# Attention block on one core: the softmax reciprocals go through DRAM, and VectorE divides out of PSUM

## The chip, the cores and the metric

The kernel runs on one core of a Trainium2 chip. A core has TensorE (PE, matrix products into PSUM), VectorE (DVE), ScalarE (ACT) and GpSimd (POOL), each with its own instruction stream, and SyncE (SP), which here issues all DMAs from one queue in its written order. The engines meet only at semaphores. The metric is the device time of one execution in microseconds. Three runs of the kernel before took 717.3, 717.02 and 719.97 us; the median is 717.3 us.

## The reference

```python
q = (x @ Wq.T).reshape(B, N, 12, 32); k = (x @ Wk.T).reshape(...); v = (x @ Wv.T + bv).reshape(...)
a = einsum('bnhd,bmhd->bhnm', q, k) * SCALE + adj[:, None]     # adj is the bias of all heads
a = where(all(a == 0, axis=-1)[..., None], -inf, a)            # rows of zeros count as empty
a = nan_to_num(softmax(a, axis=-1))
o = einsum('bhnm,bmhd->bnhd', a, v).reshape(B, N, 384)
out = layernorm(x + (o @ Wo.T + bo), axis=-1)                  # B = 32 batches, N = 256 rows, float32
```

The softmax denominator is applied after the product with v: `o` is first computed with unnormalised exponentials and then multiplied by the reciprocal of each row's sum.

## The kernel before, in words

There are 32 independent batches of 256 rows and 384 columns, 12 heads of 32 columns. Every large float32 product is done as three products of a high and a low part (hi·hi, hi·lo, lo·hi). The order on each engine is written out by hand in three functions: `start()` (batches 0 to 2 and the beginning of 3), `step(t)`, run once for each batch in the middle, and `end()`. Engines work on neighbouring batches at once: t is the batch of a step, `prev`, `prev2`, `nxt` and `nxt2` are those one or two before or after it.

Pieces of one batch on TensorE, by the names used below:

- **K** blocks, three a batch: `project_kq` (K01, K2Q0, Q12), 18 matmuls of 256 columns each, into bank_c or bank_b.
- **V** blocks, two a batch: `project_v`, 9 matmuls of 384 columns into bank_b; **Y** blocks, two a batch: `project_y`, the output projection, the same shape from `o_hi`, `o_lo`.
- **S** blocks, three a batch: `scores(t, g)` for four heads each, into the four s_banks. VectorE then adds the bias and negates (`add_bias(t, u)`, L1192: units u = 0 to 11, two instructions each), and ScalarE takes the exponentials and the row sums (`exps`, L559).
- **T** blocks, four a batch: `transposes` of units 8 to 11 by the identity into bank_t, copied out by ScalarE (`copy_probT`). Units 0 to 7 are turned by VectorE in 32x32 squares (`square`, L1209), stored to DRAM and loaded again in turned order (`store_squares`, `load_squares`, 1 MB each, one pair for each of the head groups 0 and 1).
- **W** blocks, three a batch: `weigh(t, g)`, exponentials times v for head group g, into the first half of bank_a. All three groups use the same place, so each must be emptied before the next begins.
- **flag**: one small product that tells whether any row maximum is zero; VectorE reads it (`read_flag`, L1240), and `mask` (L1248) loads it into a register and branches over code that is not needed.

The reciprocals before: VectorE takes the 24 reciprocals of each partition, 12 heads by two halves of the rows (`invert`, L1264), GpSimd widens them to 32 columns each (`widen_inv`, L418), and TensorE turns them by six transposes (`spread`, L858: four into bank_c, two into bank_t). ScalarE copies each W result out of bank_a (`save_o`, L576), and VectorE multiplies that copy by the spread reciprocals in two instructions (`divide`, L1273). bank_a is free as soon as ScalarE has copied it (semaphores `o_saved`). Then `split_o_hi` (ScalarE) and `split_o_lo` (GpSimd) make the parts for Y, `residual` and `moments` (VectorE), `deviation` (GpSimd) and `normalise` (ScalarE) finish the batch.

Of the kernel before, what the change touches and what calls it, by code (L numbers as in the profile page):

```python
# [13 lines left out]
P = 128  # L14
# [66 lines left out]
def build(nc, x, xT, adj, wqT, wkT, wvT, bv, woT, bo, out):  # L81
    def sb(name, shape, dt=F32):
# [23 lines left out]
    sums = [sb(f"sums{p}", [P, NT, H]) for p in range(2)]  # L106
# [15 lines left out]
    most = sb("most", [P, NT, H])  # L122
    inv = sb("inv", [P, NT, H])
    inv_wide = sb("inv_wide", [P, NT, H, HD])
    o_raw = [sb(f"o_raw{p}", [P, KC, N]) for p in range(2)]
    o_n = sb("o_n", [P, KC, N])
# [19 lines left out]
    bank = {"R0": bank_c, "K01": bank_c, "Q12": bank_c, "PV0": bank_a, "PV1": bank_a, "PV2": bank_a,  # L146
            "K2Q0": bank_b, "V0": bank_b, "V1": bank_b, "Y0": bank_b, "Y1": bank_b}
    t_flat = bank_t[:].rearrange("p k m q -> p (k m q)")
    bank["R1"] = t_flat
    flags_at = bank_a[:, N:N + NT * H]  # L150
# [3 lines left out]
    last_bank = {"R0": s_flat[0], "Y0": s_flat[0], "R1": s_flat[1], "Y1": s_flat[1], "PV1": s_flat[2], "PV2": bank_c[:]}  # L154
# [42 lines left out]
    o_saved = [sem(f"o_saved{g}") for g in range(KC)]  # L197
# [4 lines left out]
    inv_wide_ready = sem("inv_wide_ready")  # L202
    inv_spread = sem("inv_spread")
# [11 lines left out]
    CONSTS = 4  # L215
# [7 lines left out]
    with nc.Block() as block:  # L223

        @block.sync
        def _(sp):
# [32 lines left out]

            def store_out(t):  # L260
# [27 lines left out]
            def start():  # L288
                t0 = Batch(0)
                t1 = Batch(1)  # L290
                t2 = Batch(2)
                t3 = Batch(3)
                t4 = Batch(4)
                load_bias(t1)
                load_xt(t2)
                load_xr(t0)
                store_squares(t0, 0)
                load_xr(t1)
                load_squares(t0, 0)
                load_xt(t3)  # L300
                store_squares(t0, 1)
                load_xt(t4)
                load_squares(t0, 1)
                load_bias(t2)
                store_squares(t1, 0)
                store_squares(t1, 1)
                load_squares(t1, 0)
                load_squares(t1, 1)
                load_bias(t3)
                store_squares(t2, 0)  # L310
                load_squares(t2, 0)
                load_xr(t2)
                store_squares(t2, 1)
                load_bias(t4)
                load_squares(t2, 1)
                store_squares(t3, 0)
                store_out(t0)

            def step(t):
                nxt2 = t.later(2)  # L320
                nxt = t.later(1)
                prev2 = t.later(-2)
                load_xt(nxt2)
                load_bias(nxt2)
                load_squares(t, 0)
                store_squares(t, 1)
                load_squares(t, 1)
                load_xr(t)
                store_squares(nxt, 0)
                store_out(prev2)  # L330

            def end():
                t28 = Batch(28)
                t29 = Batch(29)
                t30 = Batch(30)
                t31 = Batch(31)
                store_squares(t30, 1)
                load_squares(t30, 0)
                load_squares(t30, 1)
                store_squares(t31, 0)  # L340
                load_xr(t30)
                load_squares(t31, 0)
                store_squares(t31, 1)
                store_out(t28)
                load_squares(t31, 1)
                store_out(t29)
# [5 lines left out]
            for c in range(3, 30):  # L352
                step(Batch(c))
# [4 lines left out]
        def _(pool):  # L358
# [3 lines left out]
            pool.wait_ge(const_ready, 3)  # L362
# [41 lines left out]
            def split_o_lo(t, k):  # L404
# [5 lines left out]
                nc.gpsimd.tensor_tensor(o_lo[:, a:b], o_n[:, a:b], o_hi[:, a:b].bitcast(F32), ALU.subtract  # L410
                                        ).then_inc(o_ready, 1)

            def widen_inv(t):
                pool.wait_ge(inv_ready, t.count(1, 1))

                after(pool, inv_spread, t.count(2))
                apart(pool)
                nc.gpsimd.tensor_copy(inv_wide[:], inv[:].unsqueeze(3).to_broadcast([P, NT, H, HD])  # L418
                                      ).then_inc(inv_wide_ready, 1)
# [19 lines left out]
            def start():  # L439
# [9 lines left out]
                split_kq(t0, "Q12")  # L449
                permute_bias(t1)  # L450
                split_kq(t1, "K01")
                split_xt(t2)
                split_kq(t1, "K2Q0")
                split_kq(t1, "Q12")
                split_kq(t2, "K01")
                widen_inv(t0)
                split_kq(t2, "K2Q0")
                split_kq(t2, "Q12")
                permute_bias(t2)
                split_xt(t3)  # L460
                add_bo(t0)
                split_xt(t4)
                split_o_lo(t0, 0)
                split_kq(t3, "K01")
                split_o_lo(t0, 1)
                widen_inv(t1)
                split_kq(t3, "K2Q0")
                permute_bias(t3)
                add_bo(t1)
                split_kq(t3, "Q12")  # L470
                deviation(t0)
                widen_inv(t2)
                split_o_lo(t1, 0)
                split_kq(t4, "K2Q0")

            def step(t):
# [4 lines left out]
                permute_bias(nxt)  # L481
                split_o_lo(prev2, 1)
                split_kq(nxt, "K01")
                add_bo(prev)
                split_xt(nxt2)
                split_kq(nxt, "Q12")
                deviation(prev2)
                split_kq(nxt2, "K2Q0")
# [1066 lines left out]
```

## Time and profile before

| | |
|---|---|
| median of three runs | 717.3 us |
| the profiled execution's own time | 718.51 us |
| span of the profile | 716.2 us |
| PE busy, of the span | 698.7 us (98%) |
| DVE busy | 600.1 us (84%) |
| ACT busy | 613.8 us (86%) |
| POOL busy | 487.2 us (68%) |
| DMA packets, share of the 16 engines | 72.3% on SP's queue |
| HBM traffic | 256 GB/s over the span |

The span is the first to the last instruction; the execution's own time is 2.3 us more. PE's busy time counts pipelined matmuls, which overlap, so its work is best read as the distance from one block's start to the next block's start. The rows below have times in us from the span's start. In the timeline, the first number is the start, the second the time busy, and brackets hold idle time before the row and what ended it.

### The profile page before, as it was taken

To read this page: it belongs to the slowest core of one execution; us is meant where nothing else is said; L and a number is where in the kernel's file an instruction comes from. 1 tells how busy PE (TensorE), PEld (TensorE's weight loads), DVE (VectorE), ACT (ScalarE), POOL (GpSimd) and SP (SyncE) were. 2 spreads that over 40 slices of the span, in tenths; PEclk is the share of its full clock that TensorE was granted. 3 is DMA by queue.
4 is the path that set the end of the run, shared out by engine and by line. 5 is a ranking of instruction groups with operands and counts; after the bars stand their busy time and mean duration, and the time that the engine had idled before them with its cause. 6 is when DMAs were issued, how large, how long until landed. Compare 5 with 4: busy or idle time off the path is not lost.

```text
span 716.2 us, 23143 instructions
## 1 busy us (share of the span) xinstructions
PE 698.7 (98%) x7557; PEld 600.7 (84%) x7557; DVE 600.1 (84%) x2220; ACT 613.8 (86%) x1993; POOL 487.2 (68%) x548
## 2 busy tenths in 40 slices
PE   8999999999999999999999999999999999999895
PEld 8878888888888888888888888888898888888774
DVE  4898988889888889888889888889888889888973
ACT  4889988889988889988888988889888888898882
POOL 4767666677766678766677766678766677766452
PEclk9999999999999999999999999999999999999998
DMA  8475877787777687777787777787777777777672
GB/s 266 152 278 206 300 267 264 252 315 236 263 263 273 241 309 240 265 264 267 251 302 240 262 267 259 252 305 247 257 270 261 262 291 248 255 273 259 248 288 90
DMA packets 84008, 184.61 MB, mean 258 GB/s; under 512 B 4272, under 2 KB 42928, under 8 KB 75696
## 3 DMA queue, kind: packets, MB, share of 16 engines
q1 hardware_dynamic: 83888, 183.12, 72.3%
q8 instruction: 61, 1.00, 0.6%
q14 instruction: 59, 0.48, 0.2%
HBM read 103.42 MB, written 79.69 MB: 256 GB/s over the span
## 4 chain that ended last, share of the span: by engine, by line
PE 85%; DVE 5%; DMA 4%; issue 2%; POOL 2%; ACT 1%; SPq 0%; DVEq 0%; ACTq 0%; POOLq 0%
PE bank_b L787 34%; PE bank_c L787 16%; PE bank_a L877 12%; PE s_bank L836 11%; PE bank_t L847 8%; PE bank_c L858 2%; DVE neg L1192 2%; DMA sq_dram<-w_f 2%; DMA sq_probT<-sq_dram 2%; ACT prob L559 1%; PE bank_t L858 1%; DVE w_f L1209 1%; DMA xt<-in_xT 1%; POOL kq_lo L400 0%; DVE y L1292 0%
## 5 line engine op out<-in xcount | busy, mean ns | idle before, releaser
L559 ACT ACTIVATE prob<-neg,negmax 128x256 f32<-128x256 f32 x768 | 380.3, 500 | 51.8 <-DVE w_f L1209 34.3
L1192 DVE CUSTOM_DVE_ANT_0 neg<-s_bank,bias_sq 128x256 f32<-128x256 f32 x512 | 185.2, 414 | 49.0 <-issue 42.6
L1209 DVE STREAM_TRANSPOSE w_f<-prob 128x512 f32<-128x512 f32 x256 | 173.2, 696 | 0.7 <-ACT prob L559 0.7
L559 ACT ACTIVATION_READ_ACCUMULATOR prob<-neg,negmax 128x1 f32 x768 | 147.7, 192 | 0.0
L400 POOL TENSOR_TENSOR kq_lo<-kq,kq_hi 128x512 fp32r<-128x512 f32 x96 | 125.2, 1304 | 7.7
L398 POOL CAST kq_hi<-kq 128x512 fp32r<-128x512 f32 x96 | 60.2, 627 | 79.3 <-issue 73.9
L787 PE MATMUL bank_c<-xt_hi,w_hi 128*128 128x256 f32 x384 | 111.1, 289 | 1.0 <-DVE w_lo L1171 1.0
L787 PE MATMUL bank_c<-xt_hi,w_lo 128*128 128x256 f32 x384 | 108.3, 282 | 0.0
L787 PE MATMUL bank_c<-xt_lo,w_hi 128*128 128x256 f32 x384 | 108.3, 282 | 0.0
L1192 DVE CUSTOM_DVE_ANT_0 neg<-s_bank,bias 128x256 f32<-128x256 f32 x256 | 91.0, 420 | 15.2 <-PE s_bank L836 15.0
L847 PE MATMUL bank_t<-ident,prob 128*128 128x128 f32 x512 | 80.3, 279 | 0.7 <-ACT probT L569 0.7
L569 ACT ACTIVATE probT<-bank_t 128x512 f32<-128x512 f32 x128 | 75.0, 586 | 3.6 <-PE bank_t L847 2.9
L787 PEld LDWEIGHTS bank_c<-xt_hi,w_hi 128*128 128x128 f32 x384 | 73.0, 190 | 2.1 <-issue 1.7
L410 POOL TENSOR_TENSOR o_lo<-o_n,o_hi 128x512 fp32r<-128x512 f32 (+1 forms) x62 | 63.4, 1025 | 15.4 <-ACT o_hi L584 15.4
L787 PEld LDWEIGHTS bank_c<-xt_hi,w_lo 128*128 128x128 f32 x384 | 73.1, 190 | 0.0
L787 PEld LDWEIGHTS bank_c<-xt_lo,w_hi 128*128 128x128 f32 x384 | 73.1, 190 | 0.0
L877 PE MATMUL bank_a<-sq_probT,v 128*32 128x256 f32 x1008 | 67.5, 385 | 1.2 <-DVE zero_flag L1240 1.0
L787 PE MATMUL bank_b<-w_hi,o_hi 128*128 128x384 f32 x186 | 68.3, 367 | 0.3 <-DVE y L1292 0.3
L787 PE MATMUL bank_b<-w_hi,xt_hi 128*128 128x384 f32 x192 | 67.8, 353 | 0.3 <-ACT kq L542 0.2
L836 PE MATMUL s_bank<-kq_hi 32*128 32x256 f32 x768 | 65.2, 328 | 2.6 <-POOL kq_lo L400 1.3
L836 PEld LDWEIGHTS s_bank<-kq_hi 32*128 32x128 f32 x768 | 37.3, 183 | 34.4 <-issue 33.3
L847 PEld LDWEIGHTS bank_t<-ident,prob 128*128 128x128 f32 x512 | 56.5, 140 | 10.7 <-issue 1.6
(88 smaller groups left out, 1794.1 us busy)
## 6 DMA issues: line engine op xcount, KB each, us to landing
sq_dram<-w_f SPq DMA_DIRECT2D x64, 1024.0 KB, 4.5
sq_probT<-sq_dram SPq DMA_DIRECT2D x64, 1024.0 KB, 5.6
xt<-in_xT SPq DMA_DIRECT2D x32, 384.0 KB, 4.5
xr<-in_x SPq DMA_DIRECT2D x32, 384.0 KB, 6.2
out_y<-y_out SPq DMA_DIRECT2D x31, 384.0 KB, 3.0
bias<-in_adj SPq DMA_DIRECT2D x32, 256.0 KB, 3.2
w_f<-in_wkT SPq DMA_DIRECT2D x3, 192.0 KB, 4.5
w_f<-in_wqT SPq DMA_DIRECT2D x3, 192.0 KB, 5.0
```

The costliest lines, as they stand in the source:

```text
L398: nc.gpsimd.tensor_copy(kq_hi[t.p][:, a:a + 2, :], kq[:, a:a + 2, :]).then_inc(kq_hi_ready[name], 1)
L400: nc.gpsimd.tensor_tensor(kq_lo[t.p][:, a:a + 2, :], kq[:, a:a + 2, :], kq_hi[t.p][:, a:a + 2, :].bitcast(F32), ALU.subtract).then_inc(kq_ ...
L410: nc.gpsimd.tensor_tensor(o_lo[:, a:b], o_n[:, a:b], o_hi[:, a:b].bitcast(F32), ALU.subtract).then_inc(o_ready, 1)
L559: nc.scalar.activation(prob[:, u % PROB_RING, k], neg[:, h, w.c], ACT.Exp, scale=-1.0, bias=negmax[t.p][:, w.c, h:h + 1], accum_out=sums[t ...
L569: nc.scalar.activation(probT[:, a:a + PAIR, :, P * w.c:P * (w.c + 1)], bank_t[:], ACT.Copy).then_inc(probT_act, 1)
L787: last = nc.tensor.matmul(ps, w_pair[a](k), m_pair[b](k), start=(k == 0 and e == 0), stop=(k == KC - 1 and e == 2))
L836: last = nc.tensor.matmul(s_bank[j][:, c, :], a[t.p][rows, KC + g, P * c:P * (c + 1)], b[t.p][rows, g, :], start=(e == 0), stop=(e == 2))
L847: last = nc.tensor.transpose(bank_t[:, k, m, :], prob[:, u % PROB_RING, k, P * m:P * (m + 1)], ident[:])
L858: last = nc.tensor.transpose(bank_at(t, f"R{k}")[:, at:at + P], inv_wide[:, c, JH * g:JH * (g + 1), :].rearrange("p h d -> p (h d)"), iden ...
L877: last = nc.tensor.matmul(bank_at(t, f"PV{g}")[HD * j:HD * (j + 1), 0:N], v[t.p][:, m, HD * h:HD * (h + 1)], weights, start=(m == 0), stop ...
L1192: nc.vector.tensor_tensor_reduce(out=neg[:, h, w.c], in0=s_bank[h % JH][:, w.c, :], in1=by[t.p][:, w.c, :], scale=-1.0, scalar=BIG, op0=AL ...
L1209: nc.vector.transpose(sq_stage[w.g][:, :, a:a + PAIR, :, w.c].rearrange("p b h m s -> p (h m) b s"), prob[:, u % PROB_RING].rearrange("p k ...
```

## The change

The spreading of the reciprocals leaves TensorE and GpSimd. `invert` now writes the 24 reciprocals into the first columns of a 32-column tile whose rest holds ones; `turn_inv` turns that in 32x32 squares on VectorE, so that a partition holds 32 rows of one head and one row half; `store_inv` writes the 16 KB to DRAM, where the rows of one head then lie in a line; and four loads (`load_inv`), one for each head position j, repeat 768 reciprocals over 32 partitions each and fill `inv_all`. `sums` has another order of its axes to suit that.

ScalarE's copy of the W results is gone. VectorE's `divide(t, g)`, now one instruction for each of the three groups, reads bank_a itself, so bank_a is free only when VectorE has divided. `o_n` has two buffers. The flag product goes to bank_t in place of bank_a. VectorE adds the bias of v in both kernels. All hand-written orders are new: `step` runs for batches 3 to 28 in place of 3 to 29, group 0 of a batch is weighed a step later, and xT is loaded three batches ahead.

```diff
-    inv_wide = sb("inv_wide", [P, NT, H, HD])
-    o_raw = [sb(f"o_raw{p}", [P, KC, N]) for p in range(2)]
-    o_n = sb("o_n", [P, KC, N])
+    inv = sb("inv", [P, SQ])
+    inv_t = sb("inv_t", [P, SQ])
+    inv_dram = [nc.dram_tensor(f"inv_dram{p}", (SQ, BLOCKS, SQ), F32, kind="Internal").ap() for p in range(2)]
+    inv_all = [sb(f"inv_all{p}", [P, KC, N]) for p in range(2)]
+    o_n = [sb(f"o_n{p}", [P, KC, N]) for p in range(2)]
...
-    flags_at = bank_a[:, N:N + NT * H]
+    flags_at = t_flat[:, 0:NT * H]
...
+            def store_inv(t):
+                sp.wait_ge(inv_turned, t.count(1, 1))
+                apart(sp)
+                after(sp, inv_loaded[t.p], JH * (t.loads() - DMA))
+                sp.dma_start(inv_dram[t.p].rearrange("k b r -> b k r"),
+                             inv_t[:]).then_inc(inv_stored[t.p], DMA)
+
+            def load_inv(t):
+                sp.wait_ge(inv_stored[t.p], t.loads())
+                apart(sp)
+                after(sp, o_n_ready, t.count(KC, -KC))
+                for j in range(JH):
+                    row = inv_dram[t.p][KC * NT * j:KC * NT * (j + 1)].rearrange("k b r -> (k b r)")
+                    sp.dma_start(inv_all[t.p][HD * j:HD * (j + 1)].rearrange("p g n -> p (g n)"),
+                                 row.rearrange("(a n) -> a n", a=1).to_broadcast([HD, KC * N])
+                                 ).then_inc(inv_loaded[t.p], DMA)
...
-            def widen_inv(t):
...
-            def save_o(t, g):
...
-            def spread(t, k):
...
             def invert(t):
                 dve.wait_ge(prob_ready, t.count(H * NT, H * NT))
-                after(dve, inv_wide_ready, t.count(1))
-                nc.vector.reciprocal(inv[:], sums[t.p][:]).then_inc(inv_ready, 1)
-
-            def divide(t, k):
-                a, b = ((0, 2), (2, 3))[k]
-                for g in range(a, b):
-                    dve.wait_ge(o_saved[g], t.count(1, 1))
-                after(dve, o_ready, t.count(2))
-                dve.wait_ge(inv_spread, t.count(2, k + 1))
-                nc.vector.tensor_tensor(o_n[:, a:b, :], o_raw[t.p][:, a:b, :],
-                                        bank_at(t, f"R{k}")[:, 0:N * (b - a)].rearrange("p (a n) -> p a n", n=N),
-                                        ALU.mult).then_inc(o_n_ready, 1)
+                dve.wait_ge(const_ready, CONSTS)
+                after(dve, inv_turned, t.count(1))
+                nc.vector.reciprocal(inv[:, 0:H * NT], sums[t.p][:].rearrange("p j g c -> p (j g c)")
+                                     ).then_inc(inv_ready, 1)
+
+            def turn_inv(t):
+                dve.wait_ge(inv_ready, t.count(1, 1))
+                if t.c >= 1:
+                    dve.wait_ge(inv_stored[1 - t.p], t.later(-1).loads())
+                apart(dve)
+                nc.vector.transpose(inv_t[:], inv[:]).then_inc(inv_turned, 1)
+
+            def divide(t, g):
+                dve.wait_ge(pv_done[g], t.count(1, 1))
+                if g == 0:
+                    dve.wait_ge(inv_loaded[t.p], JH * t.loads())
+                    after(dve, o_ready, t.count(2, -2))
+                    apart(dve)
+                nc.vector.tensor_tensor(o_n[t.p][:, g, :], bank_at(t, f"PV{g}")[:, 0:N], inv_all[t.p][:, g, :],
+                                        ALU.mult).then_inc(o_n_ready, 1)
...
-            for c in range(3, 30):
+            for c in range(3, 29):
                 step(Batch(c))
```

Of `widen_inv` (GpSimd), `save_o` (ScalarE) and `spread` (TensorE), which are removed whole, only the first line is shown here; their bodies are printed above.

**SP, one step, before** (the DMA queue, from the store of the second squares; `sq_dram` and `sq_probT` are the squares' store and load, the waits are semaphores):

```order
L248 DMA sq_dram<-w_f 128x2048 [waits squared,sq_loaded1]
L257 DMA sq_probT<-sq_dram 128x4x512 [waits sq_stored1,pv_done1]
L241 DMA xr<-in_x 128x2x384 [waits y_saved]
L248 DMA sq_dram<-w_f 128x2048 [waits squared,sq_loaded0]
L268 DMA out_y<-y_out 128x2x384 [waits y_ready]
L231 DMA xt<-in_xT 128x3x256 [waits xt_ready]
L236 DMA bias<-in_adj 128x2x256 [waits neg_ready]
L257 DMA sq_probT<-sq_dram 128x4x512 [waits sq_stored0,pv_done0]
```

**SP, one step, now:**

```order
L252 DMA sq_dram<-w_f 128x2048 [waits squared,sq_loaded0]
L235 DMA xt<-in_xT 128x3x256 [waits xt_ready]
L252 DMA sq_dram<-w_f 128x2048 [waits squared,sq_loaded1]
L245 DMA xr<-in_x 128x2x384 [waits y_saved]
L261 DMA sq_probT<-sq_dram 128x4x512 [waits sq_stored0,pv_done0]
L240 DMA bias<-in_adj 128x2x256 [waits neg_ready]
L269 DMA inv_dram<-inv_t 4x32x32 [waits inv_turned,inv_loaded1]
L279 DMA inv_all<-inv_dram 32x768 [waits inv_stored1,o_n_ready]
L279 DMA inv_all<-inv_dram 32x768 x3
L261 DMA sq_probT<-sq_dram 128x4x512 [waits sq_stored1,pv_done1]
L291 DMA out_y<-y_out 128x2x384 [waits y_ready]
```

The store and the four loads of the reciprocals stand ahead of the load of the second squares of the same batch; xt, xr and bias have moved too.

**PE, around the weighing of group 1, before** (end of an S block, W, the four transposes of the spread, first matmul of Y):

```order
L836 MATMUL s_bank<-kq_hi,kq_lo 128x256 x4
L877 MATMUL bank_a<-sq_probT,v 32x256 [waits sq_loaded1,v_saved,o_saved0]
L877 MATMUL bank_a<-sq_probT,v 32x256 x7
L858 MATMUL bank_c<-ident,inv_wide 128x128 [waits inv_wide_ready,kq_saved_K01]
L858 MATMUL bank_c<-ident,inv_wide 128x128 x3
L787 MATMUL bank_b<-w_hi,o_hi 128x384 [waits o_ready,v_saved]
```

**PE, the same place now** (flag, S, W, first matmul of a K block):

```order
L916 MATMUL bank_t<-zero_max,ones 128x24 [waits zero_found,probT_act]
L880 MATMUL s_bank<-kq_hi 128x256 [waits neg_ready,kq_ready_K2Q0,kq_ready_K01]
...
L880 MATMUL s_bank<-kq_hi,kq_lo 128x256 x4
L909 MATMUL bank_a<-sq_probT,v 32x256 [waits sq_loaded1,v_saved,o_n_ready]
L909 MATMUL bank_a<-sq_probT,v 32x256 x7
L831 MATMUL bank_b<-xt_hi,w_hi 128x256 [waits xt_ready,y_saved]
```

W of group 1 now waits for `o_n_ready`, VectorE's division of group 0, where it waited for ScalarE's copy; the spread is gone.

**DVE, around the flag, before** (`TENSOR_LOAD` and the branch are `mask`):

```order
L1209 STREAM_TRANSPOSE w_f<-prob 128x4x4x32 [waits prob_ready]
L1292 TENSOR_TENSOR y<-bank_b,xr 128x384 [waits xr_ready,y_done]
L1273 TENSOR_TENSOR o_n<-o_raw,bank_t 128x256 [waits inv_spread,o_ready,o_saved2]
L1240 TENSOR_REDUCE zero_flag<-bank_a 1x1 [waits flag_done]
L1248 TENSOR_LOAD zero_flag [waits flag_read,zero_found]
L1249 COMPARE_AND_BRANCH
```

**DVE, the same place now** (`mask` follows the last row):

```order
L1271 TENSOR_SCALAR zero_max<-negmax 128x24 [waits flag_done,neg_ready]
L1323 TENSOR_TENSOR o_n<-bank_a,inv_all 128x256 [waits o_ready,pv_done0,inv_loaded1]
L1245 STREAM_TRANSPOSE w_f<-prob 128x4x4x32 [waits prob_ready,sq_stored1]
L1245 STREAM_TRANSPOSE w_f<-prob 128x4x4x32 [waits prob_ready] x2
L1276 TENSOR_REDUCE zero_flag<-bank_t 1x1 [waits flag_done]
L1341 TENSOR_TENSOR y<-bank_b,xr 128x384 [waits xr_ready,y_done]
L1245 STREAM_TRANSPOSE w_f<-prob 128x4x4x32 [waits prob_ready]
```

The division of group 0 stands ahead of four squares and waits for the loaded reciprocals; between the reading of the flag and `mask` there are now a residual and a square, where nothing stood.

## Rows read from the trace of the kernel before

**Rows 1.** Busy time by engine, four batches of 21.45 us: sum and mean.

```profile
sum 85.80, PE 85.80 PEld 73.89 DVE 73.78 ACT 75.74 POOL 61.18; mean PE 21.45 PEld 18.47 DVE 18.44 ACT 18.93 POOL 15.30
```

**Rows 2.** Waits of PE, longest first: us in total, times, longest.

```profile
PE bank_a L884 <- DVE zero_max L1235: 1.4, 2, 0.9
```

**Rows 3.** Timeline of PE, most of one batch: first rows of blocks.

```profile
403.09 0.28 PE L787 MATMUL bank_c<-xt_hi,w_hi 128*128 128x256 f32 x1
...
405.24 0.34 PE L787 MATMUL bank_b<-w_hi,xt_hi 128*128 128x384 f32 x1
...
406.90 0.39 PE L836 MATMUL s_bank<-kq_hi 32*128 32x256 f32 x4
...
407.81 1.07 PE L877 MATMUL bank_a<-sq_probT,v 128*32 128x256 f32 x16
408.82 0.66 PE L858 MATMUL bank_c<-ident,inv_wide 128*128 128x128 f32 x4
409.23 0.42 PE L787 MATMUL bank_b<-w_hi,o_hi 128*128 128x384 f32 x1
...
410.99 1.07 PE L877 MATMUL bank_a<-probT,v 128*32 128x256 f32 x16
...
412.90 0.66 PE L847 MATMUL bank_t<-ident,prob 128*128 128x128 f32 x4
413.31 0.42 PE L787 MATMUL bank_b<-w_hi,o_hi 128*128 128x384 f32 x1
...
414.98 0.19 PE L884 MATMUL bank_a<-zero_max,ones 128*128 128x24 bf16 x1
415.02 0.42 PE L858 MATMUL bank_t<-ident,inv_wide 128*128 128x128 f32 x2
415.20 0.36 PE L787 MATMUL bank_c<-xt_hi,w_hi 128*128 128x256 f32 x1
...
417.43 0.60 PE L847 MATMUL bank_t<-ident,prob 128*128 128x128 f32 x4
417.78 0.36 PE L787 MATMUL bank_b<-xt_hi,w_hi 128*128 128x256 f32 x1
...
420.02 0.60 PE L847 MATMUL bank_t<-ident,prob 128*128 128x128 f32 x4
420.55 1.07 PE L877 MATMUL bank_a<-sq_probT,v 128*32 128x256 f32 x16
```

**Rows 4.** Timeline of DVE, the same batch and the last one.

```profile
408.12 0.42 DVE L1192 CUSTOM_DVE_ANT_0 neg<-s_bank,bias 128x256 f32<-128x256 f32 x1 [0.55 <-PE s_bank L836]
...
415.86 0.40 DVE L1273 TENSOR_TENSOR o_n<-o_raw,bank_t 128x256 f32<-128x256 f32 x1
416.19 0.15 DVE L1240 TENSOR_REDUCE zero_flag<-bank_a 1x1 int32<-1x24 f32 x1
417.87 0.42 DVE L1192 CUSTOM_DVE_ANT_0 neg<-s_bank,bias_sq 128x256 f32<-128x256 f32 x1 [1.53 <-issue]
...
419.25 0.30 DVE L1264 RECIPROCAL inv<-sums 128x24 f32<-128x24 f32 x1
...
695.06 0.30 DVE L1264 RECIPROCAL inv<-sums 128x24 f32<-128x24 f32 x1 [0.60 <-ACT prob L559]
```

**Rows 5.** DMA issues of the whole program: count, KB each, median us to landing.

```profile
sq_dram<-w_f SPq DMA_DIRECT2D x64, 1024.0 KB, 4.5
sq_probT<-sq_dram SPq DMA_DIRECT2D x64, 1024.0 KB, 5.6
out_y<-y_out SPq DMA_DIRECT2D x2, 192.0 KB, 1.9
```

**Rows 6.** Timeline of SP: time that an issue takes.

```profile
415.59 0.34 SPq L248 DMA_DIRECT2D sq_dram<-w_f  x1
...
6.66 0.55 SPq L274 DMA_DIRECT2D bv_all<-in_bv  x1
```

**Rows 7.** DMA queue: packets, MB, share of 16 engines.

```profile
q1 hardware_dynamic: 83888, 183.12, 72.3%
```

More of the change, by code:

```diff
@@ L509, in end @@
                 deviation(t29)
-                widen_inv(t31)
                 deviation(t30)
@@ L515, in _ @@
             start()
-            for c in range(3, 30):
+            for c in range(3, 29):
                 step(Batch(c))
@@ L778, in _ @@
             start()
-            for c in range(3, 30):
+            for c in range(3, 29):
                 step(Batch(c))
@@ L976, in start @@
+                weigh(t1, 0)
+                scores(t2, 2)
+                pe.wait_ge(y_saved, t0.count(NT, 1))
+                project_kq(t4, "K2Q0")
+                pe.wait_ge(kq_saved["Q12"], t3.count(1, 1))
+                project_kq(t4, "K01")
+                copied(t1, 11)
+                flag(t2)
+                pe.wait_ge(o_n_ready, t1.count(KC, 1))
                 weigh(t1, 1)
-                scores(t2, 2)
-                pe.wait_ge(o_saved[1], t1.count(1, 1))
+                scores(t3, 0)
@@ L987, in start @@
[L987 to L988 removed]
+                pe.wait_ge(y_saved, t0.count(NT, 2))
+                project_v(t3, 0)
                 copied(t2, 8)
[L990 to L993 removed]
                 transposes(t2, 9)
[L995 to L996 removed]
+                scores(t3, 1)
@@ L1049, in step @@
+                pe.wait_ge(o_n_ready, prev.count(KC, 1))
+                weigh(prev, 1)
                 pe.wait_ge(y_saved, prev2.count(NT, 2))
                 project_kq(nxt2, "K2Q0")
+                pe.wait_ge(o_n_ready, prev.count(KC, 2))
+                weigh(prev, 2)
+                pe.wait_ge(flag_read, t.count(1, 1))
+                transposes(t, 8)
+                pe.wait_ge(kq_saved["K2Q0"], nxt2.count(1, 1))
+                project_v(nxt, 0)
+                scores(nxt, 1)
+                copied(t, 8)
@@ L1069, in end @@
                 t31 = Batch(31)
+                pe.wait_ge(kq_saved["K01"], t30.count(1, 1))
+                project_kq(t30, "Q12")
+                scores(t29, 2)
+                copied(t28, 10)
+                transposes(t28, 11)
+                pe.wait_ge(o_n_ready, t27.count(KC, 3))
+                weigh(t28, 0)
+                pe.wait_ge(v_saved, t29.count(NT, 2))
+                project_y(t27, 0)
                 pe.wait_ge(kq_saved["Q12"], t30.count(1, 1))
                 project_kq(t31, "K01")
+                copied(t28, 11)
@@ new lines, in end @@
+                flag(t29)
+                pe.wait_ge(y_saved, t27.count(NT, 1))
+                project_y(t27, 1)
+                pe.wait_ge(o_n_ready, t28.count(KC, 1))
+                weigh(t28, 1)
+                pe.wait_ge(flag_read, t29.count(1, 1))
+                transposes(t29, 8)
+                scores(t30, 0)
+                pe.wait_ge(o_n_ready, t28.count(KC, 2))
+                weigh(t28, 2)
+                pe.wait_ge(y_saved, t27.count(NT, 2))
+                project_kq(t31, "K2Q0")
@@ L1072, in end @@
+                copied(t29, 8)
+                transposes(t29, 9)
+                scores(t30, 1)
+                copied(t29, 9)
+                transposes(t29, 10)
+                pe.wait_ge(kq_saved["K2Q0"], t31.count(1, 1))
+                project_v(t30, 0)
+                copied(t29, 10)
+                transposes(t29, 11)
                 scores(t30, 2)
-                pe.wait_ge(o_saved[0], t29.count(1, 1))
-                weigh(t29, 1)
+                pe.wait_ge(o_n_ready, t28.count(KC, 3))
@@ L1075, in end @@
+                weigh(t29, 0)
                 pe.wait_ge(v_saved, t30.count(NT, 1))
                 project_v(t30, 1)
+                pe.wait_ge(v_saved, t30.count(NT, 2))
+                project_y(t28, 0)
+                copied(t29, 11)
+                flag(t30)
+                pe.wait_ge(o_n_ready, t29.count(KC, 1))
+                weigh(t29, 1)
+                scores(t31, 0)
+                pe.wait_ge(flag_read, t30.count(1, 1))
+                transposes(t30, 8)
                 pe.wait_ge(kq_saved["K01"], t31.count(1, 1))
@@ L1078, in end @@
                 project_kq(t31, "Q12")
-                pe.wait_ge(o_saved[1], t29.count(1, 1))
-                flag(t30)
-                scores(t31, 0)
-                copied(t29, 11)
-                transposes(t30, 8)
-                pe.wait_ge(kq_saved["Q12"], t31.count(1, 1))
-                spread(t29, 0)
-                pe.wait_ge(flag_read, t30.count(1, 1))
+                pe.wait_ge(o_n_ready, t29.count(KC, 2))
                 weigh(t29, 2)
-                pe.wait_ge(v_saved, t30.count(NT, 2))
@@ L1526, in _ @@
             start()
-            for c in range(3, 30):
+            for c in range(3, 29):
                 step(Batch(c))
```

691 lines of the change are left out of this document (356 added, 335 removed).

## The prediction

> **What bounds the kernel now.** I read busy time by engine first, over four middle batches. PE is busy for all of 21.45 us a batch, ACT for 18.93, DVE for 18.44, POOL for 15.30 [rows 1]. Overlapping matmuls can make that look fuller than it is, so next the waits of PE: the longest entry is 1.4 us in the whole program [rows 2]. Between two batches nothing stops PE; it goes from block to block at its own pace. The reader is to see in its timeline that each block begins where the one before ends, and to take the distance from start to start as a block's price [rows 3]. The batch time is then the sum of the blocks of a batch, and it repeats at 21.45 us. PE bounds the kernel, and what the change takes off PE is saved, until another engine or a chain of waits is as long.
>
> **What leaves PE.** The spread costs 409.23 - 408.82 = 0.41 us for four transposes and 415.20 - 415.02 = 0.18 for two [rows 3]: 0.59 a batch. The new order also has other neighbours, and neighbours cost something, so I add up all blocks of the new step with prices of [rows 3]:
> - K: 2.15 between blocks of its kind (403.09 to 405.24), 2.24 behind a T (417.78 to 420.02). Now one stands behind T, one between Ys, and one behind a W and ahead of a W. The last I take at 2.24 plus the 0.09 that a Y pays ahead of a W (1.76 at 409.23 against 1.67 at 413.31): 2.33. Sum 6.72.
> - S: three of 0.91 (406.90). Sum 2.73. W: three of 1.00 (407.81 to 408.82, 1.01). Sum 3.00.
> - V and Y: four of 1.67, none of them now ahead of a W. Sum 6.68.
> - T: 0.41 ahead of a V twice, 0.35 ahead of a K (417.43 to 417.78), and one ahead of an S, which these rows don't have; bounds 0.35 and 0.53 (ahead of W, 420.02 to 420.55). S works on 32 rows of weights as W does on 32 columns, so I take 0.53. Sum 1.70.
> - flag: 0.04 to the next start, 0.19 by its own row; I take 0.10.
>
> That is 20.93 us a batch. The same sum over the old step gives its 21.45. So 0.52 is saved a batch, between 0.2 (each new pair of neighbours 0.1 dearer) and 0.8 (the cheapest end of each).
>
> **What DVE gets.** It held 18.44 busy, two gaps of 0.17 in the moments, and 1.53 of "issue" idle ahead of the first bias of the next batch, behind the flag [rows 1, 4]: 20.3 of 21.45. That idle is `mask`: the flag is read into a register and nothing is behind it to run. In the last batch one pair of moments (0.9) stood between, and the idle left was 0.60, ended by an exponential [rows 4]. In the new order a residual and a square (some 1.1) stand there, so I count 0.5 for `mask`. Dividing becomes three instructions of 0.40 in place of one of 0.64 and one of 0.40: +0.16 (the 0.40 read PSUM already [rows 4]; that the other operand comes from SBUF in both makes it a fair price). Turning 32 columns is new: at most a reciprocal's 0.30; I take 0.2, and 0.17 more since it waits for the reciprocal. Sum 20.3 - 1.0 + 0.16 + 0.37 = 19.8. It fits under 20.93, and even without the cover on `mask` it would be 20.9.
>
> ACT loses three copies and POOL the widening; both had 2.5 us and more to spare, so these are worth nothing by themselves. The DMA engines, 72% busy on this queue [rows 7], get 400 KB a batch on top of 3.5 MB, and the batch is shorter: about 83%. Not a bound on average, but transfers will queue more often.
>
> **What the new waits cost.** Two chains now go through DRAM each batch, and both start at DVE's turning of the reciprocals, which stands behind six biases of the next batch's second S block. Their lengths must stay under 20.93.
>
> First, W of group 1 waits for its squares, and their load now stands on SP behind the store and the four loads of the reciprocals. One round: W 1.00, K 2.33, W 1.00, T 0.41, V 1.67, S 0.91, 0.31 until DVE has the scores (407.81 to 408.12), six biases of 0.345 (417.87 to 419.25 holds four) 2.07, reciprocal and turn 0.6: 10.3 us [rows 3, 4]. Then SP: store of 16 KB, four issues, load of 1 MB. An issue is 0.34 to 0.55 [rows 6], I take 0.42, so 1.7; the load lands in 5.6 [rows 5]; handing over is 0.3. The store shows nowhere: 128 pieces of 128 bytes. Nearest below is the 192 KB store with 1.9 us, and nothing here speaks for less; above is the 1 MB store with 4.5 [rows 5]. I take 2.2, near the small one. Sum 10.3 + 2.2 + 1.7 + 5.6 + 0.3 = 20.1. That is 0.8 under PE's 20.93, so it costs nothing, but every 0.1 beyond 3.0 us of store is 0.1 us a batch, and from 3.5 us on the whole gain is gone.
>
> The Trainium skill, page DMA: Bandwidth & Descriptors, section Anatomy of one DMA, gives a DMA a fixed part of about 2.0 us and the rest by bytes at 436 GB/s. By that the store would be 2.0 us (the formula is for the GpSimd path), and the round 19.9; no row here has so small a transfer.
>
> Second, DVE's own division of group 0: from the turn to it there are ten biases, 3.45, four squares of 512 columns (more than the 0.40 of 256 columns [rows 4], at most twice that; 0.6 each), v and a residual of 384 columns (0.5 each) and the zero test (0.3): some 7.1. The reciprocals need 2.2, three issues 1.3, the last load (96 KB, taken at 2.3, between the 1.9 and the 4.5) and 0.3: 6.1. It stays behind cover; DVE has 1.1 of room beyond. The load comes in time for bank_a too: DVE divides group 0 some 2 us before PE wants that place.
>
> **The sum.** 26 steps of 0.52 are 13.5 us. The other six batches lose their spread, 0.59 each: 3.5. At the end the last reciprocals can't be hidden whole: store, loads and hand-over (6.1) stand where 0.8 of widening and 0.41 of spread stood. About 3 of it lie beside the last Y and W blocks, so I charge 2.0. Net 13.5 + 3.5 - 2.0 = 15.0. From the profiled execution's own 718.5 us (span 716.2 and 2.3 around it) that is 703.5; the median of the runs lies 1.2 lower, so 702 us.
>
> **Rivals.**
> 1. PE's sum stays the bound, as above: 702 us, own range 694 to 709. For it: no wait on PE in 26 steps [rows 2], and the room that both chains have. Against: room of 0.8 us on a chain with three DMAs in a row. Chance 0.55.
> 2. The chain over SP is a little longer than PE's sum: store 3.0 to 3.5, or the 1 MB load late because transfers queue. The period is 20.93 to 21.45 and the time 702 to 716; middle 709. For it: the load of the squares starts right behind 384 KB of reciprocals. Chance 0.20, mostly still faster by more than 0.5%.
> 3. The store of the reciprocals is slow, and the kernel slower than before. One mechanism: 128 pieces of 128 bytes, landing in more than 3.5 us, each batch, on SP between turn and second squares; PE stands ahead of W of group 1. With the 4.5 us of a 1 MB store the round is 22.4 us: 26 x (22.4 - 21.45) = +25, less 1.5 at the ends, 741 us. Against: the bytes are a sixty-fourth. Chance 0.12.
> 4. DVE is the bound: `mask` is not covered (+1.0) and turn or divisions are dearer by 0.2 to 0.4. Period 21.1 to 21.3, time 706 to 711. For it: each register load stops DVE's stream. Chance 0.08.
> 5. The new neighbours and the end eat the gain: within 0.5%, 714 to 721. Chance 0.05.
>
> To rival 3 belongs a rule of the Trainium skill, DMA: Bandwidth & Descriptors, sections Specifications and Why a DMA increments its semaphore by 16 and not by 1: below 512 B a write is a read-modify-write, and a DMA runs on the largest number of engines, up to 16, that divides the slowest dimension of both sides. For a destination of 4 by 32 by 32 this is 4 engines, each with 32 small pieces. It gives no price for a piece, and no row here can show one.
>
> **Numbers.** 0.5% (3.6 us) is about what a measurement of this kernel can tell from no change. Faster: 0.55 + 0.17 + 0.08 = 0.80. Same: 0.05 from case 5 and 0.03 from case 2. Slower: 0.12. The range is 694 to 717: below, all neighbours cheap (0.8 x 26 = 21) and an end that gives back nothing; above, case 2 to its end. Case 3 stays outside.
>
> **What would show it.** Right: a distance of 20.9 us between the same blocks of two batches; no PE wait for `sq_probT` or `o_n` above a few tenths; the reciprocals' store landing in 2 to 3 us and idle ahead of DVE's first division near nothing; the "issue" idle behind the flag near 0.5. Wrong: W of group 1 waiting for DMA `sq_probT` in each batch (cases 2 and 3, told apart by the store's landing time); DVE without idle and PE waiting for `neg` or `o_n` (case 4); a distance of 21.2 or more without any wait on PE (case 5).

## The result and the profile after

The changed kernel takes 724.9 us, median of 20 runs (717.9 to 729.3), against 717.9 (716.4 to 720.7) for the kernel before in the same rounds. The ratio is 1.0082, with a 95% interval of 1.0061 to 1.0104 (the two medians alone give 1.0098): slower by 0.8%, where 2% faster was forecast. Two of the 20 runs (728.8 and 729.3 us) count as slow and are left out of the ratio, and the profiled execution is the longest of them (729.3 us, span 727.5), 4.4 us above the median. So the numbers below are set beside those of kernel f0 of the experiments, which has the same order on SP and differs only in the place of one division: its profiled execution took 724.65 us, next to the median, and it shows the same wait at the same place. The changed kernel also varies more, over 11 us where the kernel before varied over 4.

First the page of the changed kernel: busy time by engine, the main queue, what the last chain was made of, and the costliest of the lines that wait.

```profile
PE 691.2 (95%) x7365; PEld 593.1 (82%) x7365; DVE 612.6 (84%) x2284; ACT 585.0 (80%) x1897; POOL 463.2 (64%) x517
...
q1 hardware_dynamic: 94256, 196.24, 77.6%
...
PE 57%; DMA 22%; DVE 7%; issue 4%; SPq 4%; POOL 3%; ACT 2%; DVEq 0%; ACTq 0%; POOLq 0%
...
L909 PE MATMUL bank_a<-sq_probT,v 128*32 128x256 f32 x1008 | 68.6, 390 | 15.4 <-DMA sq_probT<-sq_dram 14.9
```

PE is no longer busy throughout: 5% of the span is idle, and 14.9 us of it stands ahead of one line, the W blocks, released by the load of the squares. Of the last chain 22% is DMA. DVE's division waits for the reciprocals only once, at the very end (3.0 us); its other waits are for PE. The new trip hurts elsewhere. The waits of PE (total, times, longest) say it in one row each, where before the longest entry was 1.4 us [rows 2]:

```profile
PE bank_a L909 <- DMA sq_probT<-sq_dram: 14.9, 15, 2.0
```

I then measured the distance from flag to flag of all 32 batches on PE's timeline. It was 21.45 us throughout the middle before. Now 10 of the 25 middle distances are 20.99 to 21.01, and the others reach up to 24.57 (mean 21.61). In four parts (us: to the third distance behind the first flag; 25 middle distances; the last three; last flag to the end):

| kernel | start | middle | last three | end | span |
|---|---|---|---|---|---|
| before | 93.2 | 536.3 | 63.0 | 23.6 | 716.2 |
| changed | 94.2 | 540.3 | 64.9 | 28.0 | 727.5 |
| f0 (below), the same order on SP | 94.3 | 538.0 | 61.8 | 28.8 | 722.9 |
| changed, no trip (below) | 92.0 | 524.8 | 63.2 | 24.9 | 704.9 |
| f2 (below) | 93.6 | 525.0 | 61.9 | 28.9 | 709.4 |

The blocks themselves are as cheap as forecast. The middle would be 25 x 20.99 = 524.8 if PE never waited; it is 15.5 over that. PE's 13 waits there for the squares sum to 12.7. Of the other 2.8 some 1.7 are the clock, shown at the end of this document. In f0 the middle is 13.2 over, and 15 waits for the squares sum to 11.6.

Where the wait comes from stands in the chain of waits. One round and the long links of the next, in order of time (start, us, what), each from a W block to the same block one batch later:

```profile
399.37 1.07 PE bank_a L909 x16
400.44 2.35 PE bank_b L831 x18
402.79 1.00 PE bank_a L909 x16
403.79 0.59 PE bank_t L891 x4
404.38 1.57 PE bank_b L831 x9
405.95 0.94 PE s_bank L880 x21
...
409.25 0.23 DVE inv L1305
...
409.64 0.22 DVE inv_t L1314
409.94 2.62 DMA inv_dram<-inv_t
412.63 0.34 SPq L279
...
414.35 1.10 SPq L279
...
415.57 6.42 DMA sq_probT<-sq_dram
...
422.13 1.07 PE bank_a L909 x16
...
432.70 1.93 DMA inv_dram<-inv_t
...
436.55 8.07 DMA sq_probT<-sq_dram
...
444.75 1.07 PE bank_a L909 x16
```

It is chain 1 of the prediction, link by link. From the W to the store takes 10.57 us (10.3 forecast). The store and hand-over take 2.7 in this round and 2.0 in the next (2.2). The issues take 2.9 and 1.8 (1.7): the same instruction takes SP 0.34 or 1.10. The load takes 6.4 and 8.1 (5.6). The rounds are 22.76 and 22.62 us, where PE's own sum is 20.99.

These two are among the longest. I took the same links from SP's and PE's timelines for all 25 middle batches:

| link, us | forecast | median | lowest to highest |
|---|---|---|---|
| W to the issue of the store | 10.3 | 10.57 | 10.56 to 12.11 |
| store and hand-over to the first load's issue | 2.2 | 2.01 | 1.99 to 2.69 |
| the four issues | 1.7 | 1.85 | 1.84 to 2.94 |
| the load of the second squares | 5.6 | 6.42 | 5.78 to 8.46 |
| hand-over to W | 0.3 | 0.14 | 0.13 to 0.78 |

The medians add up to 20.99 us, which is PE's own sum. The room of 0.8 us is gone in the ordinary batch, and whatever a batch has above its median PE waits for.

### The profile page after: what moved, and what is told of

It reads as the page before. It is cut to its first block, busy times and chain, and to the rows that moved or that the text cites. A ratio compares the mean times of both kernels' runs of the same rounds, so it can differ in the third digit from the quotient of the medians.

```text
span 727.5 us, 22765 instructions
## 1 busy us (share of the span) xinstructions
PE 691.2 (95%) x7365; PEld 593.1 (82%) x7365; DVE 612.6 (84%) x2284; ACT 585.0 (80%) x1897; POOL 463.2 (64%) x517
## 2 busy tenths in 40 slices
DMA packets 94376, 197.71 MB, mean 272 GB/s; under 512 B 10544, under 2 KB 49200, under 8 KB 86064
## 3 DMA queue, kind: packets, MB, share of 16 engines
q1 hardware_dynamic: 94256, 196.24, 77.6%
## 4 chain that ended last, share of the span: by engine, by line
PE 57%; DMA 22%; DVE 7%; issue 4%; SPq 4%; POOL 3%; ACT 2%; DVEq 0%; ACTq 0%; POOLq 0%
PE bank_b L831 25%; DMA sq_probT<-sq_dram 15%; PE bank_a L909 10%; PE bank_c L831 9%; PE s_bank L880 8%; PE bank_t L891 5%; DMA inv_dram<-inv_t 4%; DVE neg L1228 4%; SPq L279 4%; ACT prob L603 1%; DMA xt<-in_xT 1%; DMA sq_dram<-w_f 1%; POOL kq_lo L448 1%; DVE negmax L1228 1%; DMA inv_all<-inv_dram 1%
## 5 line engine op out<-in xcount | busy, mean ns | idle before, releaser
L603 ACT ACTIVATION_READ_ACCUMULATOR prob<-neg,negmax 128x1 f32 x768 | 149.6, 195 | 0.0
L448 POOL TENSOR_TENSOR kq_lo<-kq,kq_hi 128x512 fp32r<-128x512 f32 x96 | 126.7, 1320 | 7.7
L1228 DVE CUSTOM_DVE_ANT_0 neg<-s_bank,bias 128x256 f32<-128x256 f32 x256 | 94.1, 416 | 8.0 <-PE s_bank L880 7.9
L909 PE MATMUL bank_a<-sq_probT,v 128*32 128x256 f32 x1008 | 68.6, 390 | 15.4 <-DMA sq_probT<-sq_dram 14.9
L831 PE MATMUL bank_b<-w_hi,xt_hi 128*128 128x384 f32 x192 | 70.4, 366 | 0.0
L1323 DVE TENSOR_TENSOR o_n<-bank_a,inv_all 128x256 f32<-128x256 f32 x94 | 39.0, 415 | 32.3 <-PE bank_a L909 27.6
```

The costliest lines, as they stand in the source:

```text
L448: nc.gpsimd.tensor_tensor(kq_lo[t.p][:, a:a + 2, :], kq[:, a:a + 2, :], kq_hi[t.p][:, a:a + 2, :].bitcast(F32), ALU.subtract).then_inc(kq_ ...
L603: nc.scalar.activation(prob[:, u % PROB_RING, k], neg[:, h, w.c], ACT.Exp, scale=-1.0, bias=negmax[t.p][:, w.c, h:h + 1], accum_out=sums[t ...
L831: last = nc.tensor.matmul(ps, w_pair[a](k), m_pair[b](k), start=(k == 0 and e == 0), stop=(k == KC - 1 and e == 2))
L909: last = nc.tensor.matmul(bank_at(t, f"PV{g}")[HD * j:HD * (j + 1), 0:N], v[t.p][:, m, HD * h:HD * (h + 1)], weights, start=(m == 0), stop ...
L1228: nc.vector.tensor_tensor_reduce(out=neg[:, h, w.c], in0=s_bank[h % JH][:, w.c, :], in1=by[t.p][:, w.c, :], scale=-1.0, scalar=BIG, op0=AL ...
L1323: nc.vector.tensor_tensor(o_n[t.p][:, g, :], bank_at(t, f"PV{g}")[:, 0:N], inv_all[t.p][:, g, :], ALU.mult).then_inc(o_n_ready, 1)
```

## Experiments

Theory A in the expectations: the time is lost on the two chains that pass SP's single in-order queue, the squares' load behind the reciprocals' trip and the early division. Theory B: the added bytes saturate the DMA engines. The first four kernels share one set of runs of the kernel before, with a median of 718.0 us; the last four share another, 718.7.

**No trip.** Store and loads of the reciprocals are left out, and DVE multiplies by a tile of ones, so the softmax stays without its normalisation. Two fills with ones are added, DVE's waits for the store and the loads go with them, and every other instruction and its order stand.

```diff
 def store_inv(t):
-    sp.wait_ge(inv_turned, ...); ...; sp.dma_start(inv_dram[t.p]..., inv_t[:])
+    pass
 def load_inv(t):
-    sp.wait_ge(inv_stored[t.p], t.loads()); ...; four sp.dma_start(inv_all[t.p]...)
+    pass
```

> The changed kernel without the trip: reciprocals are still taken and turned, but neither stored nor loaded, and VectorE divides by a tile of ones, so the softmax is left unnormalised in this run. All orders as in the changed kernel. It prices store and loads together. Theory A: distance 21.0 in the middle, the end shorter by 2 to 4 us, 704 to 710 us, and hardly less than with the squares' load moved ahead, apart from the end. Theory B: much less than with that edit, by 5 us or more in the middle. Theory C (the new orders themselves cost the gain): still above 714.

Measured: 706.0 us, ratio 0.9826 (0.9810 to 0.9842), and all five runs within 1.9 us. All middle distances are 20.99 to 21.00. So the trip costs 18.9 us at the medians, the whole gain of PE's saving and 7 us more. Without the trip SP issues the load of the second squares some 6 us behind the W of the round, as soon as their store has landed; with it, 14.4 us behind. Against the profiled changed kernel the 22.6 us are 15.5 in the middle, 2.2 at the start, 1.8 in the last three distances and 3.1 behind the last flag.

**Squares first.** One line is moved on SP.

```diff
 load_bias(nxt2)
+load_squares(t, 1)
 store_inv(t)
 load_inv(t)
-load_squares(t, 1)
 store_out(prev2)
```

> The changed kernel with one edit on SP in each of the 26 middle steps: the load of the second squares is issued ahead of the store of the reciprocals, not behind the four loads. Theory A (the chain of waits W, S, biases, turn, store, four issues, load of the squares sets the batch time of the changed kernel, not bandwidth): the waits of PE for sq_probT vanish in the middle, the distance between batches is 21.0 us in all steps, the 15 us lost there come back and the time is 708 to 713 us. Theory B (the DMA engines are simply too full with 13 MB more): PE still waits for sq_probT or DVE for inv_all, the distance stays near 21.6 and the time within 3 us of 725.

Measured: 720.4 us, ratio 1.0037 (1.0012 to 1.0062), which is between what the two theories wanted (708 to 713, and within 3 us of 725), and far from the 706.0 without the trip. The queue's DMA share went up to 82.4%, not down, and PE's wait for the squares nearly went. DVE took its place. Its waits (total, times, longest), and those of PE:

```profile
DVE o_n L1323 <- DMA inv_all<-inv_dram: 14.6, 18, 2.2
```

```profile
PE bank_b L831 <- DVE y L1341: 5.3, 4, 2.1
...
PE bank_a L909 <- DMA sq_probT<-sq_dram: 3.6, 2, 2.5
```

So A's first half holds: the place of this one load on SP was worth about 4.5 us. The rest has become the second chain. The reciprocals now come later than DVE's division of group 0 wants them, and PE stands behind DVE. The edit itself lengthened this chain: the store of 16 KB, now issued behind a load of 1 MB, takes 2.9 to 5.4 us to the first load's issue (median 4.0), where it took 2.0 to 2.7 (median 2.0).

**Squares between.** The load stands behind the store of the reciprocals and ahead of their loads, so that SP's wait for the store hides nothing urgent.

```diff
 store_inv(t)
+load_squares(t, 1)
 load_inv(t)
-load_squares(t, 1)
```

> The changed kernel with the load of the second squares issued between the store of the reciprocals and their four loads, in the middle steps. Theory A: the squares leave 4 to 5 us earlier, so PE does not wait for them; the four loads of reciprocals now queue behind 1 MB and land 2.5 to 3 us later, which DVE feels at its first division (0 to 2 us a batch); 710 to 722 us. Theory B (DMA engines too full): as before, near 725.

Measured: 718.7 us, ratio 1.0004 (0.9983 to 1.0025). The reciprocals' loads now land in 4.7 us instead of 2.3, behind 1 MB, while the store is back at 2.0, and DVE waits for the loads 25 times:

```profile
DVE o_n L1323 <- DMA inv_all<-inv_dram: 19.9, 25, 1.7
```

**One load.** The four loads of 32 rows become one of 128 rows whose source is 4 by 32 (broadcast) by 768: fewer issues, the same bytes to SBUF.

```diff
-for j in range(JH):
-    row = inv_dram[t.p][KC * NT * j:KC * NT * (j + 1)].rearrange(...)
-    sp.dma_start(inv_all[t.p][HD * j:HD * (j + 1)]..., row...to_broadcast([HD, KC * N]))
+rows = inv_dram[t.p][0:H * NT].rearrange("(j m) b r -> j (m b r)", j=JH)
+sp.dma_start(inv_all[t.p][:]..., rows.unsqueeze(1).to_broadcast([JH, HD, KC * N]))
```

> The changed kernel with one load of 128 rows in place of the four of 32 rows. It takes three issues, 1.3 to 2.4 us, out of the chain ahead of the squares' load. Theory A: the round of the chain falls under or near 21.0, PE's waits for sq_probT fall from 15 us to under 5, 711 to 718 us. If, as the skill's rule on the number of engines says, a source of 4 by 32 by 768 runs on 4 engines with 32 pieces of 3 KB each (0.12 us a piece in the changed kernel), the load itself takes some 4 us more and DVE may wait for it. Theory B: no change, 725.

Measured: 840.2 us, ratio 1.1729 (1.1678 to 1.1781). Three issues a batch were saved and 115 us lost against the changed kernel. The expectation of 711 to 718 us was far off. It named the slow load and that DVE may wait for it; DVE waits 79.7 us for the reciprocals, and PE waits 75.8 us for the squares besides (14.9 in the changed kernel). The windows just behind its issue at 417.98 (columns: window, length, busy time of the five engines, granted clock, DMA share, GB/s) show it start alone on a quarter of the engines, 4 of 16, until the squares' load of 418.63 joins:

```profile
418.00:419.00 1.00, 1.00 (x29) 0.86 (x32) 0.89 (x2) 1.00 (x5) 0.92 (x2) 1.00 0.00 0
419.00:420.00 1.00, 1.00 (x17) 0.42 (x17) 0.78 (x5) 1.00 (x4) 1.00 (x2) 1.00 0.25 53
420.00:421.00 1.00, 1.00 (x6) 1.00 (x7) 1.00 (x5) 1.00 (x6) 0.92 (x2) 1.00 0.69 213
```

Its packets under 512 bytes are 8,624 against 10,544: 60 fewer a batch, which is 48 for three DMAs of 16 engines each and 12 more if the one that is left uses 4 instead of 16. The store counts the same way: 10,544 against the 4,272 of the kernel before is 196 more a batch, the 128 pieces, 64 for the four loads and 4 for the store. This agrees with the rule of the Trainium skill cited in the prediction (DMA: Bandwidth & Descriptors, section Why a DMA increments its semaphore by 16 and not by 1), that a DMA runs on the largest number of engines, up to 16, that divides the slowest dimension of both sides. I did not see at first that a broadcast hides a slowest dimension of 4. The squares' load, queued behind, landed in 9.9 to 11.3 us in the middle batches, where it took 5.8 to 8.5.

**Later division, with both orders (f1, f2), and alone (f0).** DVE divides group 0 behind two more squares of the next batch.

```diff
-divide(prev, 0)
 square(t, 4)
 square(t, 5)
+divide(prev, 0)
 square(t, 6)
 read_flag(t)
```

With the squares first on SP:

> The changed kernel with the load of the second squares ahead of the store of the reciprocals (middle steps), and VectorE's first division two squares later than in the changed kernel. With the squares' load moved alone, DVE waited 14.6 us in 18 batches for inv_all, and PE then for the residual. Theory A (two chains share one queue and the division stands too early for the reciprocals): two squares, 1.3 us, cover most of that wait, all middle distances are 21.0, 711 to 716 us. Theory B (DMA engines too full): the wait moves to another place, 718 to 722.

With the squares between:

> The same with the squares' load between store and loads of the reciprocals. The reciprocals land some 2 us after those of the other variant's best batches but start without waiting behind 1 MB in flight; DVE waited 19.9 us in 25 batches, at most 1.7 each. Theory A: all of it is covered by 1.3 us of squares and the room of 1.1; distances 21.0; 709 to 714 us. Theory B: 717 to 720.

With SP as in the changed kernel:

> The changed kernel with only the division moved behind two squares, SP's order as changed. Theory A: the squares' load still waits behind store and loads of the reciprocals, which start at the same place; no change beyond 2 us, 722 to 727, PE waits for sq_probT as before. Theory D (the early division holds back squares, exponentials and with them the rest): 715 or less.

Measured: 714.3 us with the squares first, ratio 0.9926 (0.9901 to 0.9952); 712.5 with the squares between, ratio 0.9911 (0.9886 to 0.9936); and 725.7 alone, ratio 1.0120 (1.0079 to 1.0161). The new order on SP alone gives back 4.5 to 6 us of the changed kernel's time, the later division alone nothing; the two together give 11 to 12 us and beat the kernel before by 0.7 and 0.9%. The order on SP pays for its gain on the second chain, and the later division takes that up. In f2 the middle is PE's own sum again, 20.99 us in nearly all batches, at a higher share of the DMA queue than in the changed kernel (82.6% against 77.6%). So Theory B falls as the cause: full DMA engines lengthen landings, but with this order no landing holds PE up in the middle. One batch of f2 on the chain of waits is all PE, each block starting where the one before ends:

```profile
304.74 1.00 PE bank_a L909 x16
305.74 2.34 PE bank_b L831 x18
308.09 1.00 PE bank_a L909 x16
309.09 0.59 PE bank_t L891 x4
...
325.73 1.00 PE bank_a L909 x16
```

and alone (f0), PE waits for the squares as in the changed kernel:

```profile
PE bank_a L909 <- DMA sq_probT<-sq_dram: 13.0, 16, 1.7
```

**The end.** On top of the squares first and the later division, DVE writes out the last two squares ahead of the division of batch 30.

```diff
 add_bias(t31, 9)
-divide(t30, 0)
 square(t31, 6)
 square(t31, 7)
+divide(t30, 0)
```

> The first of these two, and at the end the last two squares of the last batch ahead of the first division of batch 30, which stood before them and waited 0.67 us. In the changed kernel the last store of squares, the last load of squares and W follow from these squares in the chain that ends last. If that chain sets the end, the time is 0.5 to 1.5 us below the first variant; if not, the same.

Measured: 714.7 us, ratio 0.9934 (0.9910 to 0.9959), against 714.3 without it. The runs show no gain, though they would hardly tell one of 0.5 us. The division's place does not explain the longer end.

## Why the prediction was wrong

The direction was wrong, and the time lies outside the range. The step that failed is the sum of chain 1, "10.3 + 2.2 + 1.7 + 5.6 + 0.3 = 20.1 ... so it costs nothing", and in it the term of the load, 5.6 us. In the new order the load took 6.4 us at the median and up to 8.5, the issues up to 2.9 where 1.7 stood, and the chain was 21.0 at the median and up to 23 us where 20.1 was forecast. The second step that failed is the ends, forecast as a gain of 1.5 us and measured as a loss. Step by step:

- **What leaves PE: right, the saving 0.06 too large.** The undisturbed distance is 20.99 us, forecast 20.93. On the timeline K beside W takes 2.34 (2.33), T ahead of S 0.53 (0.53), the flag 0.11 (0.10). The 13.5 us of the middle came as 11.5 once the trip was out: 0.46 each over 25 distances, where I had counted 26 of 0.52.
- **DVE: right.** It does not set the time: the period is 20.99 without the trip and in f2. The idle behind the flag was 1.53 us a batch before and is 0.4 without the trip, where 0.5 was forecast (first row, 28 batches). The turn takes 0.21 us (0.2 and 0.17 of waiting forecast), a division out of PSUM 0.42 (0.40):

```profile
DVE o_n L1310 <- PE bank_a L898: 12.0, 28, 1.1
```

```profile
409.64 0.21 DVE L1314 STREAM_TRANSPOSE inv_t<-inv 128x32 f32<-128x32 f32 x1 [0.18 <-DVE inv L1305]
...
400.50 0.42 DVE L1323 TENSOR_TENSOR o_n<-bank_a,inv_all 128x256 f32<-128x256 f32 x1 [1.30 <-PE bank_a L909]
```

- **The store of the reciprocals: right.** In the middle it took 1.9 to 2.7 us where 2.2 was taken. Rival 3 had the right place and the wrong price: it wanted over 3.5 us of store, and the kernel became slower with 2.0.
- **Chain 1, the load of the squares: wrong, and it decided.** I took the landing from [rows 5], 5.6 us. That median belongs to the old order on SP: there this load had one DMA of 384 KB issued within 3 us behind it. The new order bunches the transfers. SP's timeline of one batch of the changed kernel:

```profile
432.70 0.53 SPq L269 DMA_DIRECT2D inv_dram<-inv_t  x1
434.71 1.72 SPq L279 DMA_DIRECT2D inv_all<-inv_dram  x4
436.55 0.38 SPq L261 DMA_DIRECT2D sq_probT<-sq_dram  x1
436.97 0.51 SPq L291 DMA_DIRECT2D out_y<-y_out  x1
438.28 0.34 SPq L252 DMA_DIRECT2D sq_dram<-w_f  x1
438.66 1.15 SPq L235 DMA_DIRECT2D xt<-in_xT  x1
```

  While SP waits for the turn and then for the store, it issues nothing. What has piled up behind, the squares, the output, the next squares' store and the next input, 2.8 MB, goes out within 3.3 us behind the reciprocals' loads. The DMA engines show the hole and the pile (the last two columns are DMA share and GB/s):

```profile
432.70:434.70 2.00, 2.00 (x19) 1.88 (x17) 2.00 (x7) 2.00 (x8) 1.54 (x3) 1.00 0.09 22
434.70:436.50 1.80, 1.80 (x42) 1.20 (x40) 1.43 (x5) 1.80 (x7) 1.72 (x2) 1.00 0.29 96
436.50:439.00 2.50, 2.50 (x23) 2.33 (x16) 2.50 (x12) 2.50 (x9) 2.42 (x4) 1.00 0.66 124
439.00:442.00 3.00, 3.00 (x24) 2.94 (x22) 2.96 (x9) 3.00 (x11) 2.92 (x4) 1.00 0.95 287
442.00:444.60 2.60, 1.20 (x27) 0.87 (x25) 1.88 (x5) 2.60 (x12) 1.45 (x1) 1.00 1.06 420
```

  For 2.0 us the engines stand nearly idle and for 1.8 more they are at 0.29; then they fill up, and are full from 439 until the load is in at 444.6. The median landings of the changed kernel, against 4.5 and 5.6 us before [rows 5]:

```profile
sq_dram<-w_f SPq DMA_DIRECT2D x64, 1024.0 KB, 7.6
sq_probT<-sq_dram SPq DMA_DIRECT2D x64, 1024.0 KB, 7.1
...
inv_all<-inv_dram SPq DMA_DIRECT2D x128, 96.0 KB, 2.3
```

  The 7.1 mixes two places: the squares of group 0, off this chain, land in 7.8 at the median, those of group 1 in 6.4. The reciprocals' bytes are not needed for a long landing. Without the trip, with the bytes of before, the squares' load lands in 8.3 us; there its issue at once behind its own store hides it. So the trip cost its time by where it stands on SP, ahead of this load; the longer landing used up the room that was left. Why the load lands later was not isolated. Company does lengthen a transfer: the same store of 16 KB takes 2.0 us in one place and 4.0 behind 1 MB. But it does not explain the spread from 5.8 to 8.5 us, since the same 1.8 MB were issued behind the load within 3.4 us in all 25 batches. That spread stays open.
- **The room.** The prediction said that 0.8 us of room bore three DMAs in a row, and that each 0.1 us beyond it costs 0.1 us a batch. It did, except that the excess came from the load and the issues (up to 2.9 and 1.2 above their terms). Rival 2 named this mechanism with 0.20, and was priced too cheaply: it let the store or a late load take up to 0.5 us a batch beyond PE's sum, and the mean distance is 21.6. I had written down the argument for it, "the load of the squares starts right behind 384 KB of reciprocals", and still charged the quiet landing.
- **Chain 2: right that it had room.** The forecast was 1.1 us. In the middle of the changed kernel the last of the four loads lands 0.6 to 2.4 us (median 2.1) before the division. With the squares ahead of them DVE waits in 18 or 25 of 32 batches.
- **Start and end: wrong sign.** Forecast was a net gain of 1.5 us there (3.5 less 2.0); measured is a loss of 7.4: 1.0 at the start, 1.9 in the last three distances, 4.4 behind the last flag. In f0 it is 5.0, and only the last part (5.1) is as large there. The chain behind the last squares' store, at the end of the changed kernel:

```profile
697.05 6.34 DMA sq_dram<-w_f
703.48 8.14 DMA sq_probT<-sq_dram
...
711.75 1.97 PE s_bank L909 x16
```

  Before, the same load was 5.50 us and the W behind it 1.07. Here the load took 2.6 us more and the W, at half clock, 0.9: 3.5 of the 4.4. In f0 the chain that ended last goes by the last reciprocals themselves:

```profile
696.88 4.49 DMA inv_dram<-inv_t
...
703.02 5.51 DMA inv_all<-inv_dram
```

  The forecast gave this trip 6.1 us with its issues, as in a quiet middle, and charged 2.0 of it; here it took 11.8. Without the trip 24.9 us remain behind the last flag, 3.9 less than in f0. Even so the two ends together give back what they gain (-1.2 at the start, +0.2 and +1.3 at the end), where I had counted a gain of 3.5. The edit to the end's order (f3) did not mend it; what orders it best stays open, as f2, too, takes 28.9 us behind its last flag.

## What to carry to other kernels

A landing time read from a trace belongs to the order it was read in. When a change inserts a wait on an in-order DMA queue, write down what is issued ahead of and behind each transfer in the new order, and charge the transfers with that company, not with their old median (here the store took 2.0 or 4.0 us, the load 5.6 or 6.4 and up to 8.5). 0.8 us of room over three DMAs in a row is no room. When one chain is mended on a shared queue, look at what now stands later: here the first edit gave back about half (725 to 720 or 719 us), and the other half came only when the second chain was given more cover too (714 and 712). And put the transfer that another engine waits for ahead of a wait that has nothing to do with it.

## What the runs showed of the hardware

- Some short waits of PE were followed by a stretch at half clock. In the changed kernel PE waited 1.96 us for the squares and went on at a granted clock of 0.5 (1.2 in place of 2.4 GHz) for 3.4 us; the W took 1.54 us instead of 1.07. Windows (the last three columns are granted clock, DMA share and GB/s) and the W's row:

```profile
292.00:294.00 2.00, 2.00 (x16) 1.19 (x9) 1.02 (x4) 0.00 (x0) 0.00 (x0) 0.50 1.14 432
294.00:296.00 2.00, 2.00 (x14) 2.00 (x14) 1.94 (x11) 0.00 (x0) 0.00 (x0) 0.68 0.90 275
```

```profile
291.40 1.54 PE L909 MATMUL bank_a<-sq_probT,v 128*32 128x256 f32 x16 [1.96 <-DMA sq_probT<-sq_dram]
```

  The distance of that batch is 24.57 us, 3.6 above PE's own sum: the wait, and 1.7 for the clock, half of 3.4. A wait of 1.69 us (422.13) was not followed by a lower clock. The length of one wait does not tell it alone: behind a wait of 1.90 us in f3 the clock fell (96.08), behind one of 1.98 us in f0 it stayed at 1.00 (707.25). In the one-load kernel, with waits up to 3.6 us, the mean granted clock was 0.936, against 0.997 before.
- A store of 128 pieces of 128 bytes took 1.9 to 2.7 us in the middle of the changed kernel, where 192 KB took 1.9 [rows 5]; each piece is 13 ns in the trace. The small pieces cost little here. The same store took 4.0 us (median, up to 5.4) behind a load of 1 MB, and 4.49 at the end of f0. What costs is the wait for the round trip on an in-order queue.
- The time that one DMA takes SP to issue varies, 0.34 to 1.10 us within one group of four, where 0.42 was taken from [rows 6].
